# A fused six-stage network on one core: the linear layer multiplies A x by products of weights made on the chip, cross attention's reciprocals are widened by ScalarE, and the clamped layer's VectorE order is another

## What is computed

```python
# linear attention, 16 heads of 64, scale = 1/8
q = softmax(x @ Wq, over the 64 features) * scale
k = softmax(x @ Wk, over the 32 tokens of a sequence)
v = x @ Wv
context = einsum('bhdn,bhen->bhde', k, v)
out     = einsum('bhde,bhdn->bhen', context, q) @ w_out + b_out

# cross attention, 16 heads of 8
scores = rope(q) @ rope(k).T / sqrt(8) + mask, then -1e9 where padded
out    = (softmax(scores) @ v) @ Wo.T

# clamped attention, 16 query heads and 8 key heads of 64
sim  = 50 * tanh((l2norm(q) * gq) @ (l2norm(k) * gk).T / 50) / 8
out  = (softmax(causal sim) @ v) @ Wout
```

## Time and profile before

| | |
|---|---|
| Median of 3 runs | 2432.17 us (2431.6 to 2434.42) |
| The profiled execution, its own time | 2431.76 us |
| Its span | 2429.8 us |
| Busy: PE, PEld, DVE, ACT, POOL | 2207.0, 1628.0, 1645.9, 1320.6, 1025.0 us |
| q of the linear stage's first and last unit | 139.1 and 523.7 us |
| First and last reciprocal of the cross stage (128 of them) | 1113.4 and 1742.4 us |
| First and last norm of the clamped stage (32) | 1753.2 and 2095.9 us |

### The profile page before, as it was taken

The page is one execution under the profiler, slowest core; times in us unless marked ns, Lnnn a source line. Parts: engine busy times, 40 slices in busy tenths (PEclk is TensorE's granted clock), DMA queues, the critical chain, the costliest instruction groups (busy, mean ns, idle before and its releaser), DMA issues. The chain is left out here.

```text
span 2429.8 us, 85043 instructions
## 1 busy us (share of the span) xinstructions
PE 2207.0 (91%) x30116; PEld 1628.0 (67%) x30117; DVE 1645.9 (68%) x4710; ACT 1320.6 (54%) x3760; POOL 1025.0 (42%) x925
## 2 busy tenths in 40 slices
PE   7989999989999899988999999999889999886993
PEld 4657777766888677765666666666556666664991
DVE  4577777766777543347999999999767666642441
ACT  3555555556777543335777777777555555431330
POOL 1023333325777300006555555555266666522124
PEclk8999999998999599998999999999899999978996
DMA  6630000000000000001111111111130000000112
GB/s 163 174 105 1 0 0 0 0 1 1 0 0 0 1 1 0 0 4 44 35 33 33 33 33 33 33 33 33 60 133 0 0 0 0 1 15 25 43 40 69
DMA packets 41209, 71.55 MB, mean 29 GB/s; under 512 B 6176, under 2 KB 30624, under 8 KB 40480
## 3 DMA queue, kind: packets, MB, share of 16 engines
q1 hardware_dynamic: 37792, 63.55, 8.8%
q0 software_dynamic: 3328, 6.82, 0.9%
HBM read 60.91 MB, written 9.44 MB: 29 GB/s over the span
## 5 line engine op out<-in xcount | busy, mean ns | idle before, releaser
L2211 ACT ACTIVATE xat_scores<-xat_scores,xat_least 128x257 f32<-128x257 f32 x512 | 258.7, 505 | 68.8 <-DVE xat_least L2335 68.5
L2335 DVE CUSTOM_DVE_ANT_0 xat_scores<-bank,xat_mask_b 128x257 f32<-128x257 f32 x512 | 205.5, 420 | 47.6 <-PE bank L2055 47.4
L2113 PE MATMUL bank<-ident,xat_scores 128*128 128x128 f32 x1024 | 189.0, 287 | 1.0 <-ACT xat_p_T L2224 0.6
L1011 POOL TENSOR_TENSOR gqa_rnorm<-gqa_norm_min,gqa_minus_half 128x12 f32<-128x12 f32 x64 | 145.8, 2278 | 103.6 <-DVE gqa_norm_min L1088 103.6
L2113 PEld LDWEIGHTS bank<-ident,xat_scores 128*128 128x128 f32 x1024 | 116.3, 141 | 83.0 <-issue 59.0
L656 POOL TENSOR_TENSOR lin_q_softmax<-lin_q_exp,lin_q_rsum 128x512 f32<-128x512 f32 x64 | 66.7, 1042 | 246.9 <-DVE lin_q_rsum L712 246.9
L1629 DVE SCALAR_TENSOR_TENSOR X<-bank,expert_shares,X 128x128 f32 (+1 forms) x256 | 71.8, 344 | 131.1 <-PE bank L1543 131.1
L2224 ACT ACTIVATE xat_p_T<-bank 128x256 f32<-128x256 f32 x256 | 96.0, 375 | 112.2 <-PE bank L2113 112.0
L1566 ACT ACTIVATE moe_gelu<-bank 128x512 f32<-128x512 f32 x128 | 76.4, 597 | 146.0 <-PE bank L1533 146.0
L1359 POOL TENSOR_TENSOR bat_scores<-bat_scores,bat_max 128x512 f32<-128x512 f32 x128 | 131.7, 1039 | 56.0 <-DVE bat_max L1391 54.2
L1543 PEld LDWEIGHTS bank<-moe_w,moe_gelu 128*128 128x128 f32 x1024 | 124.2, 192 | 30.8 <-issue 18.2
(11 more groups left out here) (308 smaller groups left out, 6109.7 us busy)
## 6 DMA issues: line engine op xcount, KB each, us to landing
glu_ctx_N<-in_ctxN SPq DMA_DIRECT2D x32, 576.0 KB, 4.4
xat_ctx_T<-in_ctxT SPq DMA_DIRECT2D x32, 516.0 KB, 3.5
xat_pad<-in_xat_pad SPq DMA_DIRECT2D x32, 128.5 KB, 3.3
expert_w<-in_glx_w SPq DMA_DIRECT2D x1, 4096.0 KB, 15.6
slot_rows<-gqa_zero_rows SPq DMA_DIRECT2D x1, 2560.0 KB, 11.8
slt_rows<-slot_rows SPq DMA_DIRECT2D x40, 64.0 KB
slot_results<-slt_y POOLq DMA_DIRECT2D x40, 64.0 KB, 1.8
moe_w<-in_moe_w SPq DMA_DIRECT2D x2, 1024.0 KB
```

Of the source, the lines that this page charges most:

```text
L1011: pool.tensor_tensor(rn[h][:, :], sm[h][:, :], half_neg[:, :], ALU.pow).then_inc(rnorm, 1)
L2113: m = pe.transpose(dst[:, c * P:(c + 1) * P], sx[j % 2][:, g, c * P:(c + 1) * P], k.ident[:, :])
L2211: act.activation(sx[j % 2][:, g, :], sx[j % 2][:, g, :], ACT.Exp, bias=mn[j % 2][g][:, 0:1], scale=-1.0, accum_out=sm[j % 2][:, g:g + 1]). ...
L2335: dve.tensor_tensor_reduce(sx[j % 2][:, g, :], pS[g][:, 0:J], mb[slot][:, j, :], 1.0, BIG, ALU.add, ALU.min, mn[j % 2][g][:, 0:1]).then_in ...
```

## The change

In the linear stage v is no longer made. With A the small matrix of a head, out = sum over heads of (A v) w_out = sum over heads of (A x)(Wv w_out). At the start PE turns Wv (8 transposes), DVE copies it, PE makes the 16 products Wv w_out (each 128 x 128), and ACT copies them times the scale. Then in each unit four matmuls of 32 rows x 256 columns make z = A x (`z`, in place of the 32 of `o`), ACT copies 128 x 256 four times (in place of 128 x 128 four times and v's 128 x 512), and `y` has 16 matmuls a tile, 8 in each unit. POOL keeps a copy of the normalised x (`x_kept`), and the residual of a tile is added in h = 1 instead of h = 0. In the cross stage DVE makes only the 4 reciprocals of each row, and ACT spreads them to 128 x 128 (`r_copy`); PE waits for that copy. In the clamped stage DVE does `scale` ahead of `o_norm`, and `norm` of the next tile after `qt_copy`.

```diff
             def o(t, h):
...
-                for c in range(NC):
-                    for b in range(BT):
-                        n = slice(S * b, S * b + S)
-                        for half in range(2):
-                            hd = 2 * c + half
-                            m = pe.matmul(pB[b][DH * half:DH * half + DH, c * S:(c + 1) * S],
-                                          vs[h][n, hd * DH:(hd + 1) * DH], am[h][n, hd, :], start=True, stop=True)
-                m.then_inc(o_made, 1)
+            def z(t, slot, h):
+                u = unit(t, h)
+                pe.wait_ge(x_kept, t + 1)
+                pe.wait_ge(a_copied, 2 * u + 2)
+                wait(pe, z_copied, BT * u)
+                pe.sem_inc(pe_waited, 1)
+                for b in range(BT):
+                    n = slice(S * b, S * b + S)
+                    m = pe.matmul(pZ[b][:, ZC], xk[slot][n, :], am[h][n, :, :], start=True, stop=True)
+                m.then_inc(z_made, 1)
+            def y(t, slot, h):
+                pe.wait_ge(z_copied, BT * (unit(t, h) + 1))
+                if h == 0:
+                    wait(pe, added, 2 * (t - 1) + 1)
+                for i in range(HALF):
+                    hd = HALF * h + i
+                    m = pe.matmul(pY[:, 0:D], zT[slot][:, hd, :], wvo[:, hd // 2, hd % 2, :],
+                                  start=(hd == 0), stop=(hd == H - 1))
...
+            def wv_transpose():
+                for c in range(2 * NC):
+                    pe.transpose(pZ[c // NC][:, c % NC * P:(c % NC + 1) * P],
+                                 w[:, 2, c // NC, c % NC * P:(c % NC + 1) * P], k.ident[:, :]).then_inc(wv_turned, 1)
+            def wv_out(g):
+                pe.wait_ge(wv_copied, 2)
+                for c in range(NC):
+                    for half in range(2):
+                        r = slice(DH * half, DH * half + DH)
+                        pe.matmul(pM[g][half][:, c * P:(c + 1) * P], wvT[r, NC * g + c, :], wo[r, NC * g + c, :],
+                                  start=True, stop=True).then_inc(m_made, 1)
...
+            def z_copy(t, slot, h):
+                act.wait_ge(z_made, unit(t, h) + 1)
+                wait(act, y_made, t - 1)
+                for b in range(BT):
+                    act.activation(zT[slot][:, HALF * h:HALF * h + HALF, S * b:S * b + S],
+                                   pZ[b][:, ZC].rearrange("p (g n) -> p g n", n=S), ACT.Copy).then_inc(z_copied, 1)
...
-                    act.activation(vs[h][:, :], pV[:, :], ACT.Copy, scale=SCALE).then_inc(v_copied, 1)
...
+                pool.tensor_copy(xk[slot][:, :], xn[slot][:, :]).then_inc(x_kept, 1)
...
                 for h in range(2):
                     u = unit(t, h)
+                    if h or not first:
+                        scale(*ago(t, h, 1))
                     if not first and not (h == 0 and isinstance(t, int) and t < 2):
                         o_norm(*ago(t, h, 3))
-                    if h or not first:
-                        scale(*ago(t, h, 1))
...
-                    if h == 0 and not last:
-                        norm(t + 1, 1 - slot)
                     dve.wait_ge(ssum, 2 * u + 2)
...
                     if h or not first:
                         qt_copy(*ago(t, h, 1))
+                    if h == 0 and not last:
+                        norm(t + 1, 1 - slot)
...
+            def r_copy(t, slot, j):
+                u = BT * t + j
+                act.wait_ge(recip, u + 1)
+                wait(act, no_made, u - 1)
+                act.activation(rw[j % 2][:, :, :], spread(rs[j % 2][:, :], 32), ACT.Copy).then_inc(r_spread, 1)
...
-                dve.reciprocal(rs[j % 2][:, :, :], spread(sm[j % 2][:, :], 32)).then_inc(recip, 1)
+                dve.reciprocal(rs[j % 2][:, :], sm[j % 2][:, :]).then_inc(recip, 1)
```

More of the change, by code:

```diff
@@ L475, in stage_linear_attention, with third @@
         block = ctx.enter_context(nc.Block())
+        def third(t):
+            return not isinstance(t, int) or t >= 2
         @block.sync
@@ L565, in body @@
                     kk(t, slot, h)
-                    if not first:
-                        o(t - 1, h)
-                    v(t, slot, h)
+                    if first:
+                        wv_out(h)
+                    else:
+                        if h == 0:
+                            pe.wait_ge(m_copied, 4)
+                        z(t - 1, 1 - slot, h)
+                    if h and not first:
+                        y(t - 1, 1 - slot, 0)
+                    if h == 0 and third(t):
+                        y(t - 2, slot, 1)
                     if h == 0 and not last:
                         x_transpose(t + 1, 1 - slot)
-                    if h and not first:
-                        y(t - 1, 1 - slot)
+                    if first and h:
+                        pe.wait_ge(m_copied, 2)
                     if h or not first:
@@ L586, in x_copy, with wvo_copy @@
                 act.wait_ge(turned, t + 1)
-                wait(act, v_made, 2 * (t - 2) + 2)
+                wait(act, k_made, 2 * (t - 2) + 2)
                 act.activation(xT[slot][:, :], pX[:, MC], ACT.Copy).then_inc(xt_ready, 1)
-            def o_copy(t, slot, h):
-                act.wait_ge(o_made, unit(t, h) + 1)
+            def z_copy(t, slot, h):
+                act.wait_ge(z_made, unit(t, h) + 1)
                 wait(act, y_made, t - 1)
                 for b in range(BT):
-                    act.activation(oT[slot][:, h, :, S * b:S * b + S], pB[b][:, OC].rearrange("p (c n) -> p c n", n=S),
-                                   ACT.Copy).then_inc(o_copied, 1)
+                    act.activation(zT[slot][:, HALF * h:HALF * h + HALF, S * b:S * b + S],
+                                   pZ[b][:, ZC].rearrange("p (g n) -> p g n", n=S), ACT.Copy).then_inc(z_copied, 1)
+            def wvo_copy(g):
+                for half in range(2):
+                    act.wait_ge(m_made, 2 * NC * g + 2 * NC - 1 + half)
+                    act.activation(wvo[:, NC * g:NC * g + NC, half, :], pM[g][half][:, :].rearrange("p (c n) -> p c n", n=D),
+                                   ACT.Copy, scale=SCALE).then_inc(m_copied, 1)
             def a_copy(t, h):
                 u = unit(t, h)
-                wait(act, o_made, u - 1)
+                wait(act, z_made, u - 1)
                 for half in range(2):
@@ L685, in body @@
                     norm(t, slot)
+                    for g in range(2):
+                        dve.wait_ge(wv_turned, NC * (g + 1))
+                        dve.tensor_copy(wvT[:, NC * g:NC * g + NC, :],
+                                        pZ[g][:, :].rearrange("p (c n) -> p c n", n=P)).then_inc(wv_copied, 1)
                 for h in range(2):
@@ L693, in body @@
                         k_recip(u - 1, 1 - h)
-                    if h == 0 and (not isinstance(t, int) or t >= 2):
+                    if h and third(t):
                         add(t - 2)
@@ L1988, in stage_cross_attention @@
         sm = [sb(f"p_sum{i}", [P, G]) for i in range(2)]
-        rs = [sb(f"p_rsum{i}", [P, G, 32]) for i in range(2)]
+        rs = [sb(f"p_rsum{i}", [P, G]) for i in range(2)]
+        rw = [sb(f"p_rsum_wide{i}", [P, G, 32]) for i in range(2)]
         pl = [sb(f"p_last{i}", [P, G, 32]) for i in range(2)]
@@ L2231, in body @@
                     one, two = ago(t, slot, j, 1), ago(t, slot, j, 2)
+                    if more:
+                        r_copy(*two)
                     if some:
@@ L2245, in body @@
                 if last:
+                    r_copy(t, slot, 2)
                     t_copy(t, slot, 3, 0, (0, T0))
@@ L2248, in body @@
                     v_copy(t, slot, 3, (0, VV))
+                    r_copy(t, slot, 3)
             steps(act, NT, body)
```

76 lines of the change are left out of this document (38 added, 38 removed).

## The result

The changed kernel takes 2427.65 us (median of 19 runs, 2424.67 to 2433.28), the kernel before, run beside it, 2434.03 (19 runs, 2429.26 to 2435.66). The ratio is 0.9977, with an interval from 0.997 to 0.9983: 5.6 us faster, where 3 had been forecast. The profiled execution has a span of 2425.1 us, 4.7 less than before.

What follows compares the result with a forecast made beforehand. Bounds: PE's own work in linear, PE and DVE waiting for each other in cross, PE's wait for the q copy in clamped h = 0. From 2431.76 us, -12 + 0 + 9 = -3 gives 2429, range 2416 to 2440.

Steps and rivals of the forecast that it cites:

- likeliest case: Whole kernel: all three stages go as worked out, 2429 us, own range 2422 to 2437; chance 50%.
- Linear, per tile: Linear stage, PE: v removed -1.94, y added +1.96, z for o -0.50, in sum -0.48 us a tile, -15 over 31 tiles.
- Linear, "no other engine comes due": Linear stage: ACT's larger copies and DVE's later sums don't delay PE; priced at nothing, up to +0.3 us a tile as rival.
- Linear, ends: Linear stage: eight transposes at the start 1.5 us, y and larger z copies at the end 1.5, together +3.
- Cross: Cross stage: DVE's freed reciprocal time becomes longer waiting for PE's scores, ACT's copy is hidden; 0 us, from -5 to +4.
- Clamped, h = 0: Clamped stage: norm behind the q copy delays x transpose, then scores, by +0.41 us a tile, bounds +0.15 and +0.45.
- Clamped, h = 1: Clamped stage: with scale ahead of o_norm, PE's wait for scale goes, -0.12 us a tile, from -0.15 to 0.
- The norm under POOL's power: Clamped stage: POOL's power instruction holds the norm to its end, +65 us in all, 2485 us; chance 12%.
- rival (2): Clamped h = 0 scores come no later and linear gives its 12: 2420 us, or 2410 with further gains; chance 24%.
- Rival (4): Linear stage: ACT's larger copies and DVE behind them take the pace, +0.3 us a tile, 2438 us; chance 14%.

## Why the prediction was right

It named 2429.0 us, 3 under the profiled execution; 4.7 to 6.4 were measured. The mechanism of its likeliest case held in each stage, and its sizes were off in both directions. That the sum came so near is in part luck: by the table of the result the stages missed by -3.3 (linear), -2.3 (cross) and +1.8 (clamped), and +2.9 came in a stage that nobody touched. One by one:

- **Linear, per tile**: -0.48 forecast, -0.54 measured. `v` as priced (0.96 to 1.02 each), `y` +1.91 (+1.96). The mis-sized term is `z`: 0.65 us to the next row and not the 0.54 taken from the float32 scores, so -0.28 a tile in place of -0.50. What made up for it, by luck, is a term the working didn't have: the turn of x, 0.43 and 0.38 before, is 0.20 now. With it the terms add up to -0.53. Why the turn was dear is seen only in part. In the earlier trace rows it stood behind `v`; after, 2 us of `y` stand ahead of it, and between kk and `o` it took 0.21 too. That ACT's copy of `o`, for which it waited, was the cause is the argument that fits both (at 302.28 the turn starts 0.06 us behind the end of that copy), and was not tried by itself.
- **Linear, "no other engine comes due"**: true, but for more than the reason given. I had checked DVE's busy share and ACT's copies. PE's sum was not far from another bound, the chain from q to POOL's product, 6.12 us long in both kernels (302.86 to 308.98 after). Splitting `y` lengthened the short unit from 5.3 to 5.8 us and with it the chain's slack from 0.14 to 0.65. With the same instructions and `y` unsplit the kernel is 45 us slower than before. The split is no detail of the change; it carries it.
- **Linear, ends**: +3 forecast. The eight transposes cost 1.7 (1.5 taken), the tail 0.3 (1.5 taken).
- **Cross**: the steady part 0, as forecast, and the longer wait of DVE as described. The -2.3 lie inside the bound of -5; the step had no term for the ends, where nothing covers the reciprocal (it stands ahead of the last mix on DVE) and where PE's clock was lower behind the longer idle time in most profiles.
- **Clamped, h = 0**: scores 4.40 us after q forecast, 4.41 measured, by two errors that cancel, which is luck. The copy of q comes 0.05 us earlier and not 0.16, since the norm had been standing in DVE's wait for its own sum; and the row after the turn stands 0.30 behind it and not 0.40.
- **Clamped, h = 1**: -0.12 forecast; 5.52 us in place of 5.62, so -0.10, in the units without the loop's jump, and +0.02 in those with it. Behind the wait for scale, 0.15 in the earlier trace rows, the wait for the copy of q was next (0.40 us in the changed kernel), and took most of what went. Over both kinds h = 1 is 0.04 us shorter, a third of what was taken, and the unit h = 0 is 0.46 longer (6.0 for 5.55), 0.05 more than its scores are late. So a tile costs +0.40 us and not +0.29, and +9 should have been +12 to +13; the +10.8 of the table came nearer by the short end behind the last q.
- **The norm under POOL's power** (12% for 2485 us): it didn't come. By the rule of the Trainium skill, page "SBUF — State Buffer", section "Who interferes with whom", it would have; the traces disagree for the power (0.34 us at 1916.38; 30 of the 31 norms start inside one, and all take 0.34), and agree for POOL's products of 128x512 elements and more: with such a product running 16 norms of the linear stage take 0.73 or 0.74 us in the kernel before, and that of the earlier trace rows takes 0.88. Why the power is another case stays open.
- **The other rivals**: rival (2), no delay in h = 0, fell by the order on PE. Rival (4), ACT or DVE taking the pace in the linear stage, fell too, though the unsplit `y` shows ACT's copies taking it as soon as PE has nothing to do beside them.

## What to carry to other kernels

A change that moves the time by 0.2% can be three changes, here of about -15, -2 and +13 us; time each part by itself before one of them is thrown away with the others. Here the fastest kernels are those without the third. In a pipeline whose units alternate between long and short, look for the longest chain of waits through the short one before work is shared out: it decides how short that unit can get, whatever the sum of PE's work. An instruction that stands in the wait of an engine for its own result is nearly free (0.05 us for a norm of 0.34 here); before it is moved away, look whether anything queued on another engine's list, ahead of the critical work, waits for it.

## What the runs showed of the hardware

- An idle PE can pay twice: at the end of the cross stage the same eight matmuls took 1.16 us behind 1.18 us of idle time in four of four profiles, and 1.85 to 2.08 behind 1.64 in seven of nine (1.59 and 1.16 in the other two); and in the linear stage with `y` in one piece waits of 1.42 us were followed by rows at a granted clock of 0.51, though only in 12 of 31 tiles.
- The norm of 128x128 elements is held by POOL's products of 128x512 elements (0.73 us in place of 0.34) and isn't by its power (0.34 us, 0.37 us into a power of 2.28). With its sum over 256 columns it was met only in the other order, the norm first.
- The kernel before took 2393 us beside eight of the experiments and 2432 to 2434 elsewhere. The difference is in the last stage, of the routed experts: from its first PE row to the end of the program 237 to 240 us in those eight profiles, against 277 to 280 in the other six. PE's rows alone last 203 to 205 us against 263 to 266, and in the two slower profiles where the waits were read its products wait over 50 us for DVE (`glx_gh`), against 2 us in a faster one. What makes the chips differ in it stays open.
